# Attention over heads: summing the weighted values on two engines, one slot later

## What is computed

```python
def _L1_attn_ref(x, Wq, Wk, Wv, Wo, bo):
    N_HEADS = 16
    N, S, D = x.shape
    H = N_HEADS
    hd = D // H
    q = (x @ Wq.T).reshape(N, S, H, hd).transpose(0, 2, 1, 3)
    k = (x @ Wk.T).reshape(N, S, H, hd).transpose(0, 2, 1, 3)
    v = (x @ Wv.T).reshape(N, S, H, hd).transpose(0, 2, 1, 3)
    att = jnp.einsum('nqhd,nkhd->nhqk', q, k)
    att = jax.nn.softmax(att / jnp.sqrt(jnp.asarray(hd, x.dtype)), axis=3)
    out = jnp.einsum('nhqk,nkhd->nqhd', att, v).reshape(N, S, D)
    return out @ Wo.T + bo
x = x + _L1_attn_ref(_layernorm(x, axis=-1), ...)
```

## Time and profile before

| | us |
|---|---|
| median of 3 runs | 3264.93 |
| lowest and highest run | 3261.05 and 3267.3 |
| span of the profiled execution (first to last instruction) | 3260.9 |
| this stage in it, first to last instruction | 1807.2 to 2269.0 |

### The profile page before, as it was taken

The page is one execution under the profiler, slowest core; times in us unless marked ns, Lnnn a source line. Parts: engine busy times, 40 slices in busy tenths (PEclk is TensorE's granted clock), DMA queues, the critical chain, the costliest instruction groups (busy, mean ns, idle before and its releaser), DMA issues. The chain is left out here.

```text
span 3260.9 us, 77410 instructions
## 1 busy us (share of the span) xinstructions
PE 2876.7 (88%) x24966; PEld 2373.3 (73%) x24967; DVE 2258.3 (69%) x4939; ACT 1998.5 (61%) x4307; POOL 1809.3 (55%) x3200
## 2 busy tenths in 40 slices
PE   5999999799999999959897799997589999999996
PEld 4666666588888888858786577776367777777775
DVE  4777777467666766545554699997777878787643
ACT  3555555466666666534443466665487777777762
POOL 2223232255666666624555677774576868676752
PEclk9999999799999999979999899998599999999998
DMA  4444444200000000022222100000000000000000
GB/s 131 138 134 122 128 137 134 78 2 6 13 13 13 13 12 13 16 82 76 73 73 67 36 0 0 0 0 1 1 1 5 5 8 5 8 5 8 8 5 10
DMA packets 205069, 128.65 MB, mean 39 GB/s; under 512 B 14256, under 2 KB 197528, under 8 KB 204184
## 3 DMA queue, kind: packets, MB, share of 16 engines
q1 hardware_dynamic: 196632, 108.57, 11.8%
q0 software_dynamic: 8192, 16.79, 1.8%
HBM read 34.82 MB, written 90.51 MB: 38 GB/s over the span
## 5 line engine op out<-in xcount | busy, mean ns | idle before, releaser
L1547 POOL TENSOR_TENSOR a_qk<-a_qkv 128x2048 f32<-128x2048 f32 x64 | 235.3, 3676 | 58.4 <-ACT a_qkv L1522 54.4
L1480 PE MATMUL a_ps_s<-a_qk,w_ident 128*128 128x256 f32 x1024 | 238.3, 387 | 27.5 <-POOL a_qk L1547 27.3
L960 POOL TENSOR_TENSOR x_p<-x_p,x_rz 128x1232 f32<-128x1232 f32 x64 | 143.9, 2248 | 170.8 <-DVE x_rz L1069 170.8
L1480 PEld LDWEIGHTS a_ps_s<-a_qk,w_ident 128*128 128x128 f32 x1024 | 193.2, 194 | 57.3 <-issue 23.0
L199 POOL TENSOR_TENSOR a_four<-stats 128x4 f32<-128x4 f32 (+1 forms) x47 | 9.6, 204 | 384.3 <-DVE stats L529 272.4
L1529 ACT ACTIVATE a_r<-a_o,w_a_rows 128x128 f32<-128x128 f32 x512 | 220.9, 523 | 2.1 <-DVE a_o L1579 2.1
L1338 POOL DMA_INDIRECT f_yg<-f_rows_out,f_index x128 | 122.8, 960 | 176.3 <-DVE f_yo L1418 159.0
L2196 POOL TENSOR_TENSOR x_sq<-x_e 128x1232 f32<-128x1232 f32 x64 | 143.3, 2240 | 129.1 <-DVE x_t_sq L2355 128.9
L512 DVE TENSOR_REDUCE a_nmax<-a_ps_s 128x4 f32<-128x512 f32 x256 | 159.0, 684 | 41.8 <-PE a_ps_s L317 41.8
L421 ACT ACTIVATE a_e<-a_ps_s 128x512 f32<-128x512 f32 x256 | 153.0, 602 | 24.0 <-PE a_ps_s L333 24.0
L1076 DVE TENSOR_REDUCE x_top<-x_ps_s 128x16 f32<-128x1232 f32 x64 | 91.3, 1426 | 109.0 <-PE x_ps_s L700 108.9
(11 more groups left out here) (559 smaller groups left out, 9749.3 us busy)
## 6 DMA issues: line engine op xcount, KB each, us to landing
f_rows_in<-a_zeros SPq DMA_DIRECT2D x31, 1088.0 KB, 5.4
f_rows_out<-a_zeros SPq DMA_DIRECT2D x31, 1088.0 KB, 8.8
f_xin<-f_rows_in SPq DMA_DIRECT2D x135, 64.0 KB
f_rows_out<-f_yo SPq DMA_DIRECT2D x135, 64.0 KB
out<-x SPq DMA_DIRECT2D x16, 256.0 KB
f_raw<-in_late_f SPq DMA_DIRECT2D x2, 1408.0 KB, 6.0
w_ctx<-in_ctx SPq DMA_DIRECT2D x1, 2464.0 KB
f_rows_in<-f_xr,f_where POOLq DMA_INDIRECT x128
```

The lines of the kernel that those rows point to most:

```text
L960: nc.gpsimd.tensor_tensor(wide, wide, rz[:, :].unsqueeze(2).broadcast_to([P, HEADS, K]), ALU.mult).then_inc(p_ready, 1)
L1480: ins = nc.tensor.matmul(ps_s[u % 2][:, 0:HEADS * HEADS], c.ident[:, :], qk[:, u % 2, k, :, :], start=k == 0, stop=k == HD - 1)
L1547: nc.gpsimd.tensor_tensor(qk[:, u % 2, :, :, :], qkv[:, u, 0, :, :].unsqueeze(3).broadcast_to(full), qkv[:, u, 1, :, :].unsqueeze(2).broad ...
```

## The change

The sum over 16 heads is made in two parts. The GpSimd adds `ev` of heads 0 to 7 and `ev` of heads 8 to 15 into a new tile `pairs` (128x1024), in the slot in which `ev` is made. The VectorE sums the remaining eight a slot later (a new stage SUM = 6), into a PSUM tile of its own, and makes `o` then. `ev`, `pairs` and `rz` get two buffers. The ScalarE's spread stays in stage 6, the output projection in stage 7. exp now waits for `ev` and `z` of two steps before in the place of `o`.

```diff
@@ -1437,20 +1437,22 @@
         qkv = sb("qkv", [P, UNROLL, 3, HD, HEADS])
         qk = sb("qk", [P, 2, HD, HEADS, HEADS])
         top, dif = sb("top", [P, HEADS]), sb("dif", [P, 2, HEADS, HEADS])
-        z, rz = sb("z", [P, HEADS]), sb("rz", [P, HEADS])
-        ev = sb("ev", [P, HEADS, HD, HEADS])
+        z, rz = sb("z", [P, HEADS]), sb("rz", [P, 2, HEADS])
+        ev = sb("ev", [P, 2, HEADS, HD, HEADS])
+        pairs = sb("pairs", [P, 2, HEADS, HD, HEADS // 2])
         o = sb("o", [P, 2, HEADS, HD])
         r = sb("r", [P, 2, HD, HEADS, A])
         ps_x, ps_qkv, ps_y = ps("ps_x"), ps("ps_qkv"), ps("ps_y")
         ps_s = [ps(f"ps_s{i}") for i in range(2)]
         ps_e = [ps(f"ps_e{i}") for i in range(2)]
-        names = ("xn_ready", "xT_ps", "xT_ready", "qkv_ps", "qkv_ready", "qk_ready", "s_ps", "top_done", "dif_ready", "exp_done",
+        ps_sums = ps("ps_sums")
+        names = ("paired", "xn_ready", "xT_ps", "xT_ready", "qkv_ps", "qkv_ready", "qk_ready", "s_ps", "top_done", "dif_ready", "exp_done",
                  "z_done", "rz_done", "ev_done", "sums_done", "o_ready", "r_ready", "y_ps", "x_done", "biased")
-        (xn_ready, xT_ps, xT_ready, qkv_ps, qkv_ready, qk_ready, s_ps, top_done, dif_ready, exp_done,
+        (paired, xn_ready, xT_ps, xT_ready, qkv_ps, qkv_ready, qk_ready, s_ps, top_done, dif_ready, exp_done,
          z_done, rz_done, ev_done, sums_done, o_ready, r_ready, y_ps, x_done, biased) = (sem(n) for n in names)
         block = ctx.enter_context(nc.Block())
 
-        TURN, PROJECT, MULTIPLY, SCORE, WEIGH, SPREAD, LAST = 1, 2, 3, 4, 5, 6, 7
+        TURN, PROJECT, MULTIPLY, SCORE, WEIGH, SUM, SPREAD, LAST = 1, 2, 3, 4, 5, 6, 6, 7
         LAG = LAST
         full = [P, HD, HEADS, HEADS]
         final_in = sem("final_in")
@@ -1466,8 +1468,7 @@
         def weights_of(u):
             return ps_e[u % 2][:, 0:HEADS * HEADS].rearrange("p (i j) -> p i j", i=HEADS)
 
-        def sums_of(u):
-            return ps_e[u % 2][:, HEADS * HEADS:HEADS * HEADS + D].rearrange("p (i d) -> p i d", i=HEADS)
+        sums = ps_sums[:, 0:D].rearrange("p (i d) -> p i d", i=HEADS)
 
         @block.tensor
         def _(pe):
@@ -1532,7 +1533,8 @@
                 if at := sl.step(SCORE):
                     s, u = at
                     act.wait_ge(dif_ready, s + 1)
-                    wait(act, o_ready, s - 1)
+                    wait(act, ev_done, s - 1)
+                    wait(act, z_done, s - 1)
                     nc.scalar.activation(weights_of(u), dif[:, u % 2, :, :], ACT.Exp, scale=HD ** -0.5).then_inc(exp_done, 1)
 
             run_slots(act, slot, B, LAG)
@@ -1546,6 +1548,12 @@
                     wait(pool, s_ps, s - 1)
                     nc.gpsimd.tensor_tensor(qk[:, u % 2, :, :, :], qkv[:, u, 0, :, :].unsqueeze(3).broadcast_to(full),
                                             qkv[:, u, 1, :, :].unsqueeze(2).broadcast_to(full), ALU.mult).then_inc(qk_ready, 1)
+                if at := sl.step(WEIGH):
+                    s, u = at
+                    pool.wait_ge(ev_done, s + 1)
+                    wait(pool, sums_done, s - 1)
+                    nc.gpsimd.tensor_tensor(pairs[:, u % 2, :, :, :], ev[:, u % 2, :, :, 0:HEADS // 2], ev[:, u % 2, :, :, HEADS // 2:HEADS],
+                                            ALU.add).then_inc(paired, 1)
                 if at := sl.step(TURN):
                     s, u = at
                     pool.wait_ge(xn_ready, s + 1)
@@ -1566,17 +1574,20 @@
                     s, u = at
                     n = [P, HEADS, HD, HEADS]
                     dve.wait_ge(exp_done, s + 1)
-                    nc.vector.tensor_tensor(ev[:, :, :, :], weights_of(u).unsqueeze(2).broadcast_to(n),
+                    wait(dve, paired, s - 1)
+                    nc.vector.tensor_tensor(ev[:, u % 2, :, :, :], weights_of(u).unsqueeze(2).broadcast_to(n),
                                             qkv[:, u, 2, :, :].unsqueeze(1).broadcast_to(n), ALU.mult).then_inc(ev_done, 1)
                     nc.vector.tensor_reduce(z[:, :], weights_of(u), AX.X, ALU.add).then_inc(z_done, 1)
                     dve.wait_ge(z_done, s + 1)
-                    nc.vector.reciprocal(rz[:, :], z[:, :]).then_inc(rz_done, 1)
-                    dve.wait_ge(ev_done, s + 1)
-                    nc.vector.tensor_reduce(sums_of(u), ev[:, :, :, :], AX.X, ALU.add).then_inc(sums_done, 1)
+                    nc.vector.reciprocal(rz[:, u % 2, :], z[:, :]).then_inc(rz_done, 1)
+                if at := sl.step(SUM):
+                    s, u = at
+                    dve.wait_ge(paired, s + 1)
+                    nc.vector.tensor_reduce(sums, pairs[:, u % 2, :, :, :], AX.X, ALU.add).then_inc(sums_done, 1)
                     dve.wait_ge(rz_done, s + 1)
                     dve.wait_ge(sums_done, s + 1)
                     wait(dve, r_ready, s - 1)
-                    nc.vector.tensor_tensor(o[:, u % 2, :, :], sums_of(u), rz[:, :].unsqueeze(2).broadcast_to([P, HEADS, HD]),
+                    nc.vector.tensor_tensor(o[:, u % 2, :, :], sums, rz[:, u % 2, :].unsqueeze(2).broadcast_to([P, HEADS, HD]),
                                             ALU.mult).then_inc(o_ready, 1)
                 if at := sl.step(SCORE):
                     s, u = at
```

## The result

The changed kernel takes 3369.99 us (median of 4 runs, 3368.84 to 3375.3), the kernel before 3262.99 beside it (3253.23 to 3267.3): ratio 1.0335, interval 1.0316 to 1.0354, 107 us slower. The forecast was 3352, ratio 1.027, and 3325 to 3385 as its range: right in sign and in the cause of the larger part, and short by a fifth in size. The profiled execution spans 3366.6 us, 105.7 more than before.

The account below looks back on a forecast made before the run. The VectorE was taken to set the pace at 6.84 us a slot, then a VectorE-ScalarE loop at 8.22: 61 x 1.38 = 84.2, + 0.7 + 2.1 = 87.0 on 3260.9, plus 4.0 to the median: 3352 us, range 3325 to 3385.

Parts of the forecast that it names:

- The loop: VectorE and ScalarE: `ev`, sum, `o`, spread, exp, next `ev` run one after the other, 8.22 us a slot, 1.38 more.
- the bounds that the sum's own terms gave: Whole kernel: total time with the reduction's bounds, 3347 to 3366 us.
- a term put at nothing: GpSimd: backlog from the chain of four, 6 us once in four slots, taken to cost nothing.
- The VectorE's saving: VectorE's sum: 1024 fewer elements per partition save 1.04 us, bounds 0.81 to 1.12.
- the loop's head in one of four slots: Loop: measured mean 0.08 us above the plain slot, put down to one slot in four; 0.03 added.
- I cost the backlog at nothing: GpSimd: chain of four delays products 6 us once in four slots, but scores want them over a slot later; cost nothing.
- The addition's price: GpSimd: one addition of 1024 elements takes 1.91 us, bounds 1.84 and 2.80, from the row nearest in size.
- Rival 1, the GpSimd alone: No loop; the GpSimd's 7.5 us a slot sets the pace, +40 us, 3305 us; chance 5%.
- Rival 2, PE's clock: PE at the lower clock in half the slots, 3452 us; chance of anything above 3370: 12%.
- The 2.65 us: GpSimd: addition time over which its sum would exceed the loop's 8.22 us a slot.
- Drain: Stage's end: from last `ev` to last x 14.2 us where it was 12.1, +2.1 us.
- Filling: Stage's start: the first loop replaces an interval that was PE's, +0.7 us.

Follow-up runs that it names:

- experiment 3: Changed kernel, but the GpSimd adds only 128 of the 1024 pairs, so sums leave out most heads; ratio 1.0276 to the kernel before.
- experiment 4: Changed kernel with transpose and projection ahead of the scores in PE's slot, full addition kept; ratio 1.0272 to the kernel before.
- Experiment 2: Changed kernel with exp of step t-4 ahead of the spread of step t-6 on the ScalarE; ratio 1.0176 to the kernel before.
- experiment 5: Changed kernel without the GpSimd's addition: the VectorE sums all 16 heads itself, still a slot later; ratio 1.0488 to the kernel before.
- experiment 9: Kernel of experiment 6 with the chain of four cut into twelve parts over four slots; ratio 0.9836 to the kernel before.
- experiment 6: Changed kernel with the spread a slot later and the GpSimd adding only 128 of 1024 pairs; ratio 1.0074 to the kernel before.
- experiment 8: Changed kernel with the spread a slot later and four forms of the GpSimd's 1024-element operation in turn; 2.34 to 2.38 us or 1.89 each.
- experiment 10: Changed kernel with the spread a slot later, chain of four in twelve parts and the full addition; ratio 1.0075 to the kernel before.
- experiment 1: Changed kernel with the spread and last stage a slot later (SPREAD 7, LAST 8); ratio 1.0164 to the kernel before.

## Why the prediction was right, and where it was short

The loop was forecast with its mechanism and its length. That 3370 lies inside 3325 to 3385 is in part the width of the range: the bounds that the sum's own terms gave, 3347 to 3366, missed it, since a term put at nothing was worth 14.5 us and 4.2 came from outside the stage.

- *The VectorE's saving.* 1.04 us forecast; the sum takes 1169 ns and not 2235, 1.07. Right. The rest of its work kept its price: `ev` takes 2292 ns where it took 2275.
- *The loop through spread and exp.* Forecast 8.22 us a slot. The plain slots of the changed kernel have 8.16 to 8.33, and experiments 3 and 4, which take the late slot away in two ways, have 8.23 in the mean. Experiment 2 shows the mechanism by exchanging two steps of one engine, experiment 5 its length by putting the unshortened sum back. 61 x 1.39 = 85 us of the 107; the forecast had 84. One small term was right by luck: the 0.03 added for "the loop's head in one of four slots" rests on a misreading, as in the kernel before two slots of four are longer (6.95 and 6.97 us against 6.76), not one.
- *"I cost the backlog at nothing".* This step failed. The GpSimd's spare time was counted as a mean over four slots, but the chain of four comes in one piece, and what stands behind it are the products that PE wants for its scores. I had argued that these are wanted a slot and more later; the trace shows PE waiting 4.77 us for them, its next scores at a lower clock (6.14 and not 3.62 us), and the transpose, copies and spread late behind them. It costs 0.24 us a slot in the mean, 14.5 us in all. Experiments 3 and 4 take it away, the one by a short addition, the other by the order on PE. That the burst is its other half is read from the timeline: no run cuts the chain with the loop in place; experiment 9 shows it for the kernel of experiment 6.
- *The addition's price.* Forecast 1.91 us, inside bounds of 1.84 and 2.80; measured 2.34. I chose the row nearest in size, the 1232 elements of the earlier trace rows, and called it one with two full operands, but the second of them is broadcast. Both operands run in L952 and L1552 of the same group: (842 - 457)/180 = 2.14 ns per element, so 457 + 896 x 2.14 = 2.37 us. The Trainium skill, "GPSIMD Engine Reference", section on elementwise cycle accounting, gives an addition rate of which I made an estimate of 2.25, which was nearer than my row; it puts the rate down to two operands that share one read port, and experiment 8 agrees, with 2335 ns for two running operands and 1892 for one. The GpSimd's sum stayed under the loop either way, 7.8 us a slot in the place of 7.5. But the addition stands ahead of the chain of four, and 0.43 us of the 1.2 by which every fourth slot is late is the size of this error: some 5 us of the 14.5, an estimate that no run tests. In experiment 10 the price decides: 7.13 - 0.43 = 6.70 us a slot would have been under 6.84, also an estimate.
- *Rival 1, the GpSimd alone.* Not what happened, but what comes next: with the loop gone (experiments 1 and 2) the mean interval is 7.7 us. As the forecast said, the change would lose even so.
- *Rival 2, PE's clock.* It fell to 0.89, for a reason the forecast hadn't: in the changed kernel the low stretch lies behind the one idle time of 4.8 us in four slots, and the plain slots run at 1.00. The rival as it was put shows in experiment 5: no late products there, 9.28 us a slot, and a clock of 0.90. It cost next to nothing there, as the interval is the length of the loop, 9.28 us against 9.3 expected. The 2.65 us at which the addition would pass 8.22 is a slip: 8.22 - 3.68 - 0.46 - 5.97/4 = 2.59. At 2.34 nothing hangs on it.
- *The ends.* Drain 2.1 us as forecast, 14.2 from the last `ev` to the last x, and by its steps: `y`(62) takes 3.78 us and `y`(63) 2.02. Filling 1.0 less instead of 0.7 more. 4.2 us of the profile's difference lie ahead of the stage. The four runs of the kernel before span 14 us among themselves, so this may be no more than their spread; no experiment looks at it, and it stays open.

## What to carry to other kernels

When a result is made a slot later, look at each engine that uses it: if its user there stays in the same slot, everything written behind that user in the engine's program waits as well, and if the producer needs any of that, two engines that were overlapped run in turn. Count a relieved engine's spare time slot by slot and not as a mean: a burst of small operations that a slower neighbour has hidden becomes the bound when the neighbour gets faster, and cutting it into parts can be worth more than the relief. Half of a job handed over can win where the whole loses: the share is set by the room on the engine that takes it.

## What the runs showed of the hardware

- GpSimd, 1024 fp32 elements per partition: 2.34 to 2.38 us with two operands that run through different memory, addition or product, in runs of 8 or in one; 1.89 us where one operand stands still or both are the same.
- After an idle time of 4.77 us PE took 6.14 us for scores that take 3.62 (granted clock 0.60), and after one of 3.25 us 5.41 (0.68). With the burst gone and all else kept the granted clock of the stretch rose from 0.92 to 0.99 (experiment 6 to 9) and from 0.92 to 1.00 (1 to 10). After the idle times of 1.95 us in the changed kernel, `y` took its usual 2.05. Near 3 us the runs show both: in experiment 5 `y` took 3.44 us behind an idle time of 3.13, and 2.05 behind one of 2.93.
- A reduction on the VectorE of 1024 elements takes 1169 ns, just under the line between 415 for 256 and 2235 for 2048, which gives 1195.
